# Grouped attention in a decoder kernel: rope products in the step of their piece, a fourth buffer for the rounded outputs, the second piece behind the output product

## The reference, cut to what matters

```python
h = _rmsnorm(hidden_states, ln1_w)
q = _rope((h @ Wq).reshape(B, S, 32, 128), pos)
k = _rope((h @ Wk).reshape(B, S, 4, 128), pos)
v = (h @ Wv).reshape(B, S, 4, 128)
k, v = jnp.repeat(k, 8, axis=2), jnp.repeat(v, 8, axis=2)
scores = jnp.einsum('bqhd,bkhd->bhqk', q, k) / jnp.sqrt(128.)
attn = jax.nn.softmax(jnp.where(causal, scores, -1e9), axis=-1)
o = jnp.einsum('bhqk,bkhd->bqhd', attn, v).reshape(B, S, 32 * 128) @ Wo
x = resid + o
```

## Time and profile before

| what | value |
|---|---|
| time, median of 3 runs | 1761.63 us (1759.51 to 1761.83) |
| the profiled execution | 1762.68 us |
| its span | 1760.9 us |
| mean granted clock of TensorE | 0.89 of full speed |
| busy, share of the span | PE 81%, DVE 58%, ACT 40%, POOL 35% |

### The profile page before, as it was taken

One profiled execution on the slowest core, in us unless ns is written; L12 is line 12 of the kernel. 1 busy time (PEld: TensorE's weight loads), 2 busy tenths in 40 slices (PEclk: granted clock), 3 DMA queues, 4 the chain that ended last, 5 costly groups with the idle time before them and its releaser, 6 DMA issues. The chain is left out here.

```text
span 1760.9 us, 24199 instructions
## 1 busy us (share of the span) xinstructions
PE 1432.3 (81%) x8658; PEld 1035.9 (59%) x8690; DVE 1015.7 (58%) x1651; ACT 706.4 (40%) x1386; POOL 613.7 (35%) x549
## 2 busy tenths in 40 slices
PE   4886498879868457988678888888889968999997
PEld 3653343654368344443455666666667646888886
DVE  4763655427865447775656666676666654343343
ACT  2552200316522314666244554454444523444442
POOL 4100100000054342110645555555555433555552
PEclk8998655869989677889889999999999987999998
DMA  1000000020000010000200000000000012332331
GB/s 62 2 1 16 25 0 25 25 94 0 0 0 0 1 33 1 2 2 1 73 7 7 25 13 13 19 19 13 13 19 13 13 37 75 122 104 104 116 114 45
DMA packets 28668, 55.27 MB, mean 31 GB/s; under 512 B 5295, under 2 KB 16495, under 8 KB 28448
## 3 DMA queue, kind: packets, MB, share of 16 engines
q1 hardware_dynamic: 28576, 54.05, 9.4%
HBM read 51.67 MB, written 2.27 MB: 31 GB/s over the span
## 5 line engine op out<-in xcount | busy, mean ns | idle before, releaser
L1626 POOL TENSOR_TENSOR a_o_low<-a_o,a_o_high 128x512 fp32r<-128x512 f32 x64 | 83.2, 1299 | 172.4 <-ACT a_o_high L1923 172.4
L2322 DVE TENSOR_TENSOR e_act<-e_gated,ps 128x512 f32<-128x512 f32 x66 | 45.4, 688 | 165.2 <-POOL e_gated L2172 165.2
L2015 DVE TENSOR_REDUCE a_nmax<-ps 128x2 f32<-128x512 f32 x64 | 44.3, 692 | 165.8 <-PE ps L1746 165.8
L1617 POOL TENSOR_TENSOR a_raw<-a_prod 128x512 f32<-128x512 f32 x72 | 93.5, 1298 | 86.9 <-DVE a_prod L2008 86.9
L1923 ACT ACTIVATE a_o_high<-a_o 128x512 fp32r<-128x512 f32 x64 | 40.4, 631 | 207.3 <-PE ps L1678 198.6
L1897 ACT ACTIVATE a_shift<-ident,a_nmax 128x128 bf16<-128x128 f32 x256 | 81.9, 390 | 70.7 <-DVE a_nmax L2017 70.6
L2172 POOL TENSOR_TENSOR e_gated<-e_gate,e_wb 128x512 f32<-128x512 f32 x66 | 85.1, 1291 | 56.3 <-ACT e_gate L2255 44.9
L1678 PE MATMUL ps<-a_h_high,a_wq_high 128*128 128x512 f32 x128 | 58.3, 455 | 52.9 <-DVE a_prod L2008 51.3
L2163 POOL TENSOR_TENSOR e_we_low<-e_we,e_we_high 128x768 fp32r<-128x768 f32 x33 | 60.8, 1841 | 93.1 <-ACT e_we_high L2260 93.1
L575 DVE TENSOR_REDUCE x_nmax<-ps 128x2 bf16<-128x512 f32 x128 | 82.6, 691 | 11.6 <-PE ps L349 11.1
L1420 DVE SCALAR_TENSOR_TENSOR m_acc<-ps,m_conv_w,m_acc 128x1020 f32<-128x1020 f32 (+2 forms) x60 | 76.2, 1275 | 20.6 <-ACT m_acc L1365 19.2
(11 more groups left out here) (420 smaller groups left out, 4406.2 us busy)
## 6 DMA issues: line engine op xcount, KB each, us to landing
e_wb<-token_weights SPq DMA_DIRECT2D x33, 512.0 KB, 4.0
e_we<-in_experts SPq DMA_DIRECT2D x33, 384.0 KB, 3.1
a_wq<-in_a_wq SPq DMA_DIRECT2D x16, 256.0 KB, 3.0
a_wo<-in_a_wo SPq DMA_DIRECT2D x16, 256.0 KB, 2.8
m_win<-in_m_winT SPq DMA_DIRECT2D x1, 3080.0 KB
nf_raw<-in_ffn_w SPq DMA_DIRECT2D x3, 352.0 KB
ffn_deq<-nf_wout SPq DMA_DIRECT2D x3, 352.0 KB
x<-in_x SPq DMA_DIRECT2D x1, 1024.0 KB
```

Of the source, the lines that this page charges most:

```text
L1617: e.tensor_tensor(raw[:, i % 2, :], prod[:, i % 2, 0, :], prod[:, i % 2, 1, :], ALU.add).then_inc(s_raw, 1)
L1626: e.tensor_tensor(oL[:, s % 3, :], o[:, s % 2, :], oH[:, s % 3, :].bitcast(F32), ALU.subtract).then_inc(s_ol, 1)
```

## The change

The rounded outputs `oH` and `oL` get a fourth buffer (`OR = 4`), and `o_high` waits for the output product of four steps before. On DVE `rotate` takes up the piece of its own iteration, behind `residual`, where before it took up the last piece of the iteration before (and the first of its own where there are two). On POOL `add` comes to the head of the iteration, `low` to the one after the piece's. On ACT `high` is one iteration earlier too, behind `shifts`. On TensorE a step's second piece goes behind the output product.

```diff
--- before.py
+++ after.py
@@ -1491,6 +1491,7 @@
     NP = NQ // 2
     N = NP * B
     PV, PD, PO = 4, 5, 7
+    OR = 4
     P1_LONG, P1_SHORT, P2_LONG, P2_SHORT, PIECE, AV, SPREAD, OUT = range(8)
 
 
@@ -1539,7 +1540,7 @@
         shift = sb("shift", [P, 2, 4, P], BF16)
         probT = sb("probT", [P, 4, SC * 2])
         inv, invH, invS = sb("inv", [P, 2, S]), sb("inv_high", [P, 2, S], F32R), sb("inv_split", [P, 2, S], F32R)
-        oH, oL = sb("o_high", [P, 3, 2 * S], F32R), sb("o_low", [P, 3, 2 * S], F32R)
+        oH, oL = sb("o_high", [P, OR, 2 * S], F32R), sb("o_low", [P, OR, 2 * S], F32R)
 
         s_wk, s_wv, s_rot, s_mask, s_pick = (sem(n) for n in ("wk_in", "wv_in", "rot_in", "mask_in", "pick_in"))
         s_ln1 = sem("ln1_in")
@@ -1623,7 +1624,7 @@
 
         def o_low(e, s):
             e.wait_ge(s_oh, s + 1)
-            e.tensor_tensor(oL[:, s % 3, :], o[:, s % 2, :], oH[:, s % 3, :].bitcast(F32),
+            e.tensor_tensor(oL[:, s % OR, :], o[:, s % 2, :], oH[:, s % OR, :].bitcast(F32),
                             ALU.subtract).then_inc(s_ol, 1)
 
         @block.gpsimd
@@ -1654,17 +1655,17 @@
             wo_low(e, 0)
             wq_low(e, 1)
             for n in range(N + PD):
+                for i in of_step.get(n - 1, ()):
+                    add(e, i)
                 if 0 <= n - PD < N:
                     o_low(e, n - PD)
-                for i in of_step.get(n - 2, ()):
+                for i in of_step.get(n - 1, ()):
                     low(e, i)
                 p, c = n // B, n % B
                 if c == 2 and 2 <= p + 2 < NP:
                     wq_low(e, p + 2)
                 if c == 1 and 1 <= p - 1 < NP:
                     wo_low(e, p - 1)
-                for i in of_step.get(n - 1, ()):
-                    add(e, i)
 
         @block.tensor
         def _(e):
@@ -1817,7 +1818,7 @@
                 for t in range(2):
                     at = lambda j: slice(j * S + t * P, j * S + (t + 1) * P)
                     mm = three(ps[:, OUT, t * D:(t + 1) * D],
-                               [(oH[:, s % 3, at(j)], oL[:, s % 3, at(j)], woH[:, p % 2, j, :], woL[:, p % 2, j, :])
+                               [(oH[:, s % OR, at(j)], oL[:, s % OR, at(j)], woH[:, p % 2, j, :], woL[:, p % 2, j, :])
                                 for j in range(2)])
                 mm.then_inc(s_out, 1)
 
@@ -1850,10 +1851,12 @@
                 if 0 <= n - PV < N:
                     spread(n - PV)
                     values(n - PV)
-                for i in of_step.get(n, ()):
+                for i in [*of_step.get(n, ())][:1]:
                     piece(i)
                 if 0 <= n - PO < N:
                     project(n - PO)
+                for i in [*of_step.get(n, ())][1:]:
+                    piece(i)
 
         @block.scalar
         def _(e):
@@ -1918,9 +1921,9 @@
 
             def o_high(s):
                 e.wait_ge(s_o, s + 1)
-                if s >= 3:
-                    e.wait_ge(s_out, s - 2)
-                e.activation(oH[:, s % 3, :], o[:, s % 2, :], ACT.Copy).then_inc(s_oh, 1)
+                if s >= OR:
+                    e.wait_ge(s_out, s - OR + 1)
+                e.activation(oH[:, s % OR, :], o[:, s % 2, :], ACT.Copy).then_inc(s_oh, 1)
 
             const_high(0)
             e.wait_ge(s_ln1, 16)
@@ -1948,10 +1951,10 @@
             for n in range(N + PD):
                 if 0 <= n - PD < N:
                     o_high(n - PD)
-                for i in of_step.get(n - 2, ()):
-                    high(i)
                 if n < N:
                     shifts(n)
+                for i in of_step.get(n - 1, ()):
+                    high(i)
                 if 0 <= n - 1 < N:
                     exps(n - 1)
                 if 0 <= n - PV < N:
@@ -2069,10 +2072,10 @@
                     maxima(n)
                 if n % 2 and 0 <= n - 3 < N:
                     inverses((n - 3) // 2)
-                for i in [*of_step.get(n - 1, ())][-1:] + [*of_step.get(n, ())][:-1]:
-                    rotate(i)
                 if 0 <= n - PO - 1 < N:
                     residual(n - PO - 1)
+                for i in of_step.get(n, ()):
+                    rotate(i)
                 if n % 2 and 0 <= n - 3 < N:
                     split((n - 3) // 2)
```

## The result

| | time, median | runs |
|---|---|---|
| before | 1761.73 us | 4, 1759.51 to 1762.74 |
| changed | 1698.62 us | 4, 1694.43 to 1703.55 |

The ratio is 0.9641, 95% interval 0.9618 to 0.9664: 63 us less, where 50.5 were forecast. The waits went where the forecast had them go, but one term was too small, since part of the wait shows nowhere in the trace, and one loss was too large.

What follows compares the result with a forecast made beforehand. TensorE was taken as the bound, 87% busy, waiting 64.6 us for DVE's rope products. Terms 45.1 + 6.3 + 2.9 + 3 + 1 - 7.8 = 50.5 us gave 1711 us from 1761.63, range 1700 to 1727.

Steps and rivals of the forecast that it cites:

- term 1: Rope products on DVE in their piece's step: TensorE's wait goes in 28 single-piece steps, 1.61 us each, 45.1 us.
- term 4: Second piece behind output product: wait 0.97 for 2.22 us, 6.3 us over five steps, plus 2.9 from avoided half clock.
- term 2: DVE's split behind the rope products: slow in 0.4 of 27 steps at 0.72 us each, 7.8 us lost.
- expected wait of the values or the spread: Sign on TensorE: new waits for DVE's division or split, 5 to 12 us in all, in even steps only.
- term 5: First and last steps: 3 us gained in the first steps, 1 us from step 60 on.
- term 3: ACT's later rounding costs nothing, slack 1.3 us, 0.6 to 0.8 with slow split; the fourth buffer alone brings nothing.
- The rivals: Split always slow (0.15), ACT's chain late (0.12), wait only changes place (0.03), lower granted clock in the loop (0.02).
- always-slow split: Rival: DVE's split always loses to POOL's add, all 27 slow, 11.6 us more, 1723 us; chance 0.15.
- ACT's chain comes late: Rival: TensorE waits for exponentials before sums, 0.8 us in 28 odd steps, 22 us back, 1733 us; chance 0.12.
- the case without slow splits: All of DVE's splits fast, none losing to POOL's add: 1703 us, counted within the forecast's mixtures.

Runs made afterwards that it cites:

- piece_back: Changed kernel with the second piece ahead of the output product again on TensorE; 1703.1 us, 0.966 of before.
- add_second: Changed kernel with POOL's rounding of the output ahead of its add; 1697.3 us, 0.963 of before.
- rope_only: Kernel before with only DVE's rope products moved to the end of the iteration of their piece; 1697.4 us, 0.963 of before.
- even_early: Kernel before with the rope products ahead of the maxima in even iterations alone; 1761.7 us, 0.998 of before.

## Why the prediction was wrong

- **The wait goes in single-piece steps** (term 1): right in place and cause, mis-sized. "28 x 1.61 = 45.1" took the idle time of the trace for the wait. It is counted from the drawn end of the last values product, 0.59 us behind its start, while the piece can start 0.25 us behind it; the loss is 0.27 us more a step. And that in an even step the "piece starts without a wait" is wrong: it waited as well, the whole of it hidden. The 1.46 us read for the values in the earlier trace rows held that wait; they are 1.10 in the changed kernel (1123.32 to 1124.42). That is 27 x 0.25 = 6.8 us in the odd steps (1.86 measured a step, 1.61 taken), 21 x 0.28 = 5.9 in the even ones, and 2 in the two-piece steps (11.6 to 9.96 us, 1.64 a step, where term 4 had 1.25). This is the step that failed.
- **The split** (term 2): the two durations, 0.48 and 1.62, are as read, and the price of a slow one, 0.72, was 0.84. The share was not: 0.4 of 27 from a sample of three, 5 measured, and 1 to 7 in others. 4.2 us lost in place of 7.8. These 3.6 us and the 14.7 above, less the 1.2 us that term 5 fell short by, make up the 17 us by which the stretch was underrated. The expected wait of the values or the spread, 5 to 12 us, shows as 1.5 in the trace, since most of it is hidden too.
- **ACT and the fourth buffer** (term 3): right. No wait at the sums beyond the first steps but for 0.22 us at step 60, and three buffers do as well as four.
- **The second piece** (term 4): right, 0.97 forecast from the moment at which TensorE is free, 0.81 from the drawn end of the product before it; net of the longer odd step behind it, the cover is worth 1.17 us by piece_back, 1.25 forecast. The half clock is gone from these five steps, but step 6, which the term left out, fell to it where it had not before. 9.5 us came for the five steps with two slow splits among them.
- **First and last steps** (term 5): 3.7 and 0.7 us, against 4.6 and 0.7 (1 less a share of the splits, none of which was slow there). The 3.7 are after a loss to half clock of 1.5 us in step 6 and 1.1 in step 1 (granted clock 0.72 there), a matter of chance: in the third profile of the changed kernel step 6 did not fall, step 1 ran at 0.95, and the same steps took 44.0 us in place of 46.6.
- **The rivals**: none came. The always-slow split came true in single steps; "ACT's chain comes late" did happen in add_second, where the add is late, as that rival had it.
- **The range**: its lower end was built of the case without slow splits, 1703, less 2 to 3 us for first steps and the clock. It held no bound for the wait itself, which I had taken as read. The two later measurements of the changed kernel, 1693.1 and 1696.2 us, lie further below it.

## What to carry to other kernels

An idle time of zero ahead of an instruction does not say that it did not wait: compare the end of what could release it with its start, and its distance from the instruction before with the same pair elsewhere. When a late instruction is moved forward, ask each of the other moves what it does alone; here one of four carried nearly the whole gain, one did nothing, and two were only sound together with it. In this kernel two instructions that both read two SBUF tensors, one on DVE and one on POOL, ran one after the other when they started together; where one of them is on the path, give them different moments.

## What the runs showed that was not expected

- The duration that the trace draws for a float32 product of 256 columns behind another (0.59 us for the pair of line 1807) is longer than the time after which TensorE takes the next one (0.25 us). It hid waits of about 0.3 us.
- The same 0.04 to 0.05 us between split and add ended with the split first in most cases and with the add first in 1 to 7 of 32.
- Equal waits of 2.2 us are followed by half clock in some executions' steps and not in others: 2 of 5 in before and in rope_only, 4 of 5 in even_early, 3 of 5 in piece_back, and in step 6 of two of the changed kernel's three profiles. From step 7 on none fell behind a wait of 1.6 us, and no two-piece step behind one of 0.8.
